# Moving the feature load and normalisation into the edge-list stage, and moving two runs of padding instructions

## The reference

```python
h = jnp.maximum(_layernorm(x, axis=-1), 0.0)
x = x + hypergraph_layer(h, edge_index, W1, b1, W2, b2)
h = jnp.maximum(_layernorm(x, axis=-1), 0.0)
x = x + edge_layer(h, src, dst, edge_weight1, eW1, eb1, ..., nW2, nb2)

# hypergraph_layer: twice, with a relu between
e = B_inv[:, None] * segment_sum((x @ W)[node_idx], edge_idx)
out = D_inv[:, None] * segment_sum(e[edge_idx], node_idx) + b

# edge_layer
e = silu(concat([h[row], h[col], dist]) @ eW1 + eb1)
e = silu(e @ eW2 + eb2)
agg = segment_sum(e, row)
out = silu(concat([h, agg]) @ nW1 + nb1) @ nW2 + nb2
```

## Time and profile before

| what | value |
|---|---|
| three runs | 9711.72, 9714.66, 9674.4 us (median 9711.72) |
| the profiled execution: time, span | 9704.83 us, 9703.1 us |
| PE busy, share of the span | 9097.1 us, 94% |
| DVE busy | 8012.9 us, 83% |
| ACT busy | 5832.8 us, 60% |
| POOL busy | 2410.2 us, 25% |
| granted TensorE clock, mean | 0.973 of full speed |

### The profile page before, as it was taken

How to read it: one execution, slowest core, us unless ns; L and a number is a source line. 1 busy time by engine, 2 the same in 40 slices (tenths; PEclk the granted TensorE clock), 3 DMA queues, 4 the chain that set the end, 5 groups by cost and what they waited for, 6 DMA issues and landing times. The chain is left out here.

```text
span 9703.1 us, 312435 instructions
## 1 busy us (share of the span) xinstructions
PE 9097.1 (94%) x105494; PEld 8224.5 (85%) x105494; DVE 8012.9 (83%) x25426; ACT 5832.8 (60%) x14221; POOL 2410.2 (25%) x3828
## 2 busy tenths in 40 slices
PE   1999999999999999999888899679999999999997
PEld 1888888888888887999888899669999999999995
DVE  6999999999999998577598888558888888888884
ACT  1888888888888887000177788335555555555553
POOL 2555545554555453000000000001111111111110
PEclk9999999999999999999799999769999999999998
DMA  2333333333333333766499999553333333333332
GB/s 58 91 90 91 93 93 91 90 93 92 92 89 93 92 92 105 196 190 190 119 224 223 215 247 248 109 146 95 92 91 92 95 93 94 89 94 95 91 93 72
DMA packets 849659, 1149.54 MB, mean 118 GB/s; under 512 B 204300, under 2 KB 585462, under 8 KB 848004
## 3 DMA queue, kind: packets, MB, share of 16 engines
q1 hardware_dynamic: 818806, 1112.73, 43.5%
q0 software_dynamic: 28224, 26.62, 1.1%
q10 hardware_dynamic: 1840, 0.53, 0.0%
HBM read 777.40 MB, written 361.77 MB: 117 GB/s over the span
## 5 line engine op out<-in xcount | busy, mean ns | idle before, releaser
L601 POOL TENSOR_SCALAR OH<-iot,kd 128x102 bf16<-128x102 bf16 x3440 | 1973.3, 592 | 1635.5 <-DVE ddc L912 1600.5
L855 ACT ACTIVATE RB<-PS 128x512 int16<-128x512 f32 x2401 | 1408.9, 592 | 534.6 <-PE PS L721 484.7
L2136 POOL DMA_INDIRECT Qx<-tab_q,tidx x294 | 423.3, 1440 | 5170.0 <-DVE skt L2170 2586.1
L1000 DVE TENSOR_SCALAR OU<-iot,SBk 128x256 bf16<-128x256 bf16 x4802 | 1379.5, 287 | 0.0
L1391 PE MATMUL wp<-AF,XS 128*128 128x256 f32 x9604 | 1213.9, 285 | 143.0 <-issue 110.7
L1391 PEld LDWEIGHTS wp<-AF,XS 128*128 128x128 f32 x9604 | 1167.5, 191 | 172.1 <-issue 171.0
L719 PE MATMUL PS<-OU 128*128 128x256 bf16 x4802 | 1188.0, 273 | 44.1 <-DVE OU L1000 30.3
L1417 ACT ACTIVATE AF<-RG 128x1536 fp32r<-128x1536 uint8 x686 | 1022.6, 1491 | 327.1 <-PE wp L1391 264.8
L737 PE MATMUL HP<-T3a,RB 128*128 128x193 bf16 x9604 | 1192.9, 247 | 1.6 <-ACT RB L855 1.6
L721 PE MATMUL PS<-OU 128*128 128x128 bf16 x9604 | 1190.9, 219 | 0.0
L2157 ACT ACTIVATE Z<-Zb 128x512 f32<-128x512 f32 x882 | 556.3, 631 | 1022.2 <-DVE Zb L2215 1022.2
(11 more groups left out here) (326 smaller groups left out, 17602.8 us busy)
## 6 DMA issues: line engine op xcount, KB each, us to landing
RG<-adjT SPq DMA_DIRECT2D x1372, 224.0 KB, 6.0
adj<-RB SPq DMA_DIRECT2D x343, 448.0 KB, 2.6
adjT<-RB SPq DMA_DIRECT2D x686, 224.0 KB, 3.3
RG<-adj SPq DMA_DIRECT2D x686, 224.0 KB, 4.5
sdb<-bk SPq DMA_DIRECT2D x196, 768.0 KB
sdb<-bk SPq DMA_DIRECT2D x98, 384.0 KB
sdb<-bk SPq DMA_DIRECT2D x98, 261.0 KB
WR<-wk SPq DMA_DIRECT2D x882, 9.0 KB
```

Of the source, the lines that this page charges most:

```text
L601: ins = e.tensor_scalar(OH[:, g * GT + k, :], iot1[:, 0:KEYS], kd[:, g * GT + k:g * GT + k + 1], None, ALU.is_equal)
L855: e.activation(RB[n % NSLOT][:, :, k, :].bitcast(i16), bank(u)[:, :].rearrange("p (a w) -> p a w", a=2), ACT.Copy, accum_out=gs[:, u:u + 1 ...
L1000: ins = e.tensor_scalar(o[:, x_, P:3 * P], iot1[:, :], SBk[:, KEYS + b:KEYS + b + 1], None, ALU.is_equal)
```

## The change

The feature block is gone. Its load, its normalisation and its split stand in the edge block now:

- SyncE issues the two feature loads first, as soon as VectorE has zeroed the tile's corner, and the edge lists behind them.
- VectorE normalises in place in `X0` (it wrote the top of `ACC` before), and then works out the keys.
- The split is no longer VectorE's: ScalarE casts the three parts into `T3a` (three `ACTIVATE` copies), GpSimd does the two subtractions, and semaphore `l_s` passes the work back and forth between them. The values are the same.
- `junkb` and `junka` now lie in `HI` and `tb_`, which are free by then.
- `spaced(e, SPACE1)` stands in the edge block, where TensorE has nothing else; `spaced(e, SPACE2)` in the residual block, ahead of TensorE's wait for `x_v`.

```diff
+        tz = ExitStack()
+        T3af = sbt(tz, "T3a", [P, BLK * W3], bf16)
...
+            X0 = sbt(st, "X0", [P, NB, F], fp32)
...
-            junkb = sbt(st, "junkb", [P, TI], bf16)
-            junka = sbt(st, "junka", [P, TI], bf16)
+            junkb = HI
+            junka = tb_[:, 0:TI // 2].bitcast(bf16)
...
                 @block.scalar
                 def _(e):
                     load_weights(e)
+                    norm.scalar(e)
+                    v = X0[:, 0:BLK, :]
+                    e.wait_ge(norm.steps, 8)
+                    e.activation(T3a[:, :, 0:F], v, ACT.Copy).then_inc(l_s, 1)
+                    e.wait_ge(l_s, 3)
+                    e.activation(T3a[:, :, F:2 * F], v, ACT.Copy).then_inc(l_s, 1)
+                    e.wait_ge(l_s, 5)
+                    e.activation(T3a[:, :, 2 * F:3 * F], v, ACT.Copy).then_inc(l_s, 1)
+
+                @block.tensor
+                def _(e):
+                    spaced(e, SPACE1)
 
                 @block.sync
                 def _(e):
+                    e.wait_ge(l_s, 1)
+                    load_x(e, X0, l_x)
                     e.wait_ge(s_c, 3)
                     load_edges(e, E["d"], dst, s_ld)
...
                 @block.vector
                 def _(e):
+                    e.memset(eps[:, :], 1e-5)
+                    e.memset(X0[:, 97:NB, :], 0.0).then_inc(l_s, 1)
                     e.memset(E["d"][:, :], PAD).then_inc(s_c, 1)
                     e.memset(E["s"][:, :], PAD).then_inc(s_c, 1)
                     e.memset(Wt[:, :], 0.0).then_inc(s_c, 1)
-                    e.memset(eps[:, :], 1e-5)
+                    e.memset(T3a[:, :, 3 * F:W3], 1.0)
+                    e.wait_ge(l_x, 32)
+                    norm.vector(e, X0, acc64, X0[:, :, :])
                     e.wait_ge(s_fill, 1)
...
                     e.tensor_copy(idb[:, :], idn[:, :])
+                    for n in range(2):
+                        v, a = X0[:, 0:BLK, :], n * F
+                        e.wait_ge(l_s, 2 * n + 2)
+                        e.tensor_tensor(v, v, T3a[:, :, a:a + F], ALU.subtract).then_inc(l_s, 1)
                     e.iota(pio[:, :], pattern=[[P, 2]], base=1, channel_multiplier=1, allow_small_or_imprecise_dtypes=True)
...
-        def split3(link, e, to, v, rest):
-
-            link(e.tensor_copy(to[:, :, 0:F], v))
-            link(e.tensor_tensor(rest, v, to[:, :, 0:F], ALU.subtract))
-            link(e.tensor_copy(to[:, :, F:2 * F], rest))
-            link(e.tensor_tensor(rest, rest, to[:, :, F:2 * F], ALU.subtract))
-            link(e.tensor_copy(to[:, :, 2 * F:3 * F], rest))
...
-                    def _(e):
-                        e.dma_start(X[:, 0:97, :], x[0:97 * P, :].rearrange("(b p) f -> p b f", p=P)).then_inc(l_x, 16)
-                        e.wait_ge(l_s, 1)
-                        e.dma_start(X[0:N_NODES - 97 * P, 97, :], x[97 * P:N_NODES, :]).then_inc(l_x, 16)
...
-                        norm.vector(e, X, acc64)
...
-                        split3(link, e, T3a, Hn[:, 0:BLK, :], X[:, 0:BLK, :])
...
-                        spaced(e, SPACE1)
                         e.wait_ge(c_init, 4)
                         ranks(0, 0)
...
                 @block.tensor
                 def _(e):
+                    spaced(e, SPACE2)
                     e.wait_ge(x_v, 14)
                     e.matmul(pov[:, 0:1], lhsT=onef[:, :], rhs=xov[:, 0:1], start=True, stop=True).then_inc(x_v, 1)
...
                     with e.If(fits(e)):
-                        spaced(e, SPACE2)
                         e.sem_inc(l_p, OFF)
```

More of the change, by code:

```diff
@@ L318, in gnn_kernel @@
         s_k, s_km = sem("s_k"), sem("s_km")
+        tz = ExitStack()
+        T3af = sbt(tz, "T3a", [P, BLK * W3], bf16)
+        T3a = T3af[:, :].rearrange("p (b f) -> p b f", f=W3)
+        l_x, l_s = sem("l_x"), sem("l_s")
+        norm = Norm("a")
         st = ExitStack()
         with st:
+            X0 = sbt(st, "X0", [P, NB, F], fp32)
             E = {"s": sbt(st, "E_s", [P, TI], i32), "d": sbt(st, "E_d", [P, TI + 1], i32)}
@@ L444, in _ @@
                         e.matmul(pk[:, 256:257], lhsT=onef[:, :], rhs=bad[:, :], start=True, stop=True).then_inc(s_km, 1)
-        def split3(link, e, to, v, rest):
-            link(e.tensor_copy(to[:, :, 0:F], v))
-            link(e.tensor_tensor(rest, v, to[:, :, 0:F], ALU.subtract))
-            link(e.tensor_copy(to[:, :, F:2 * F], rest))
-            link(e.tensor_tensor(rest, rest, to[:, :, F:2 * F], ALU.subtract))
-            link(e.tensor_copy(to[:, :, 2 * F:3 * F], rest))
-        tz = ExitStack()
-        with tz:
[L456 to L464, removed]
-                    def _(e):
-                        e.dma_start(X[:, 0:97, :], x[0:97 * P, :].rearrange("(b p) f -> p b f", p=P)).then_inc(l_x, 16)
-                        e.wait_ge(l_s, 1)
-                        e.dma_start(X[0:N_NODES - 97 * P, 97, :], x[97 * P:N_NODES, :]).then_inc(l_x, 16)
[L470 to L474, removed]
-                        norm.vector(e, X, acc64)
[L476 to L481, removed]
-                        split3(link, e, T3a, Hn[:, 0:BLK, :], X[:, 0:BLK, :])
-                    @block.scalar
-                    def _(e):
-                        norm.scalar(e)
+        with tz:
             p1 = ExitStack()
```

## The result

| | median of 20 runs | lowest to highest |
|---|---|---|
| before | 9712.49 us | 9674.3 to 9735.65 |
| after | 9672.49 us | 9639.84 to 9680.74 |

The ratio is 0.9957 with a 95% interval of 0.9948 to 0.9965: 0.43% faster, 40.0 us by the medians, and so within the 0.5% that I had called no change. The interval is 0.17% wide, so 20 runs of each kernel do tell a difference of 0.4% from none; that "about 0.5% is what a measurement can tell" was too cautious. The forecast was 9671, from 33.7 us.

A forecast was written before the change was run, and what follows sets the result against it. TensorE bounds the long stages (busy 9097.1 of 9703.1 us), VectorE alone the program's head. Front 57.0, less 26.8 waiting, plus 3.5 padding: 33.7 us off 9704.8 gives 9671, range 9637 to 9698.

The forecast's parts named there:

- Features land: Edge block's head: feature load issued at about 1.9, 17.4 us plus 1.3 for weights' loads, landing at 20.6 us.
- Normalisation: VectorE in the edge block, behind the feature load: the same eight instructions, 39.4 us, to 60.0.
- Edge lists: Lists' loads behind the features: SyncE reaches them at 16.7, they land at about 46, costing the path nothing.
- Keys and offsets: VectorE after normalisation: keys 48.8 us, offsets block with barrier 3.9, to 112.9; waiting for GpSimd's subtractions priced at 26.8.
- the two stream counts: GpSimd subtraction's length by streams passed in turn: 10.7 us for two, 16.0 for three; the middle, 13.4, taken.
- the two kinds: Keys' long VectorE instructions: two SBUF inputs or fast one-input, expected to wait for GpSimd; only the reduction at 73.99 is neither.
- The chunk block's start: VectorE's start of the chunk block, before at 169.94: near 140 with waiting, 113 without.
- SPACE1: 136 padding increments moved from chunk block to edge block: TensorE begins 13.3 us earlier, but the gain is 3.5 us.
- SPACE2: 52 padding increments, 8.0 us, moved out of the edge-layer block: gains nothing there and hides in the new place.
- no mutual waiting: Rival for VectorE beside GpSimd's subtractions: no or little waiting, 60.5 us off, 9644; chance 0.25.
- A slow subtraction: Rival for GpSimd's subtractions: at 5.2 ns an element VectorE is held 65 us, 9710, no change; chance 0.09.
- slower: Rival for GpSimd's subtractions: each over 54.5 us, two hold VectorE or the barrier 109 us, giving -48.5; chance 0.04.

The follow-up runs named there:

- The last experiment: Changed kernel with GpSimd's two subtractions moved to VectorE between the keys' instructions, and an early ScalarE square root to load its table; median 9659.65 us, ratio 0.9946.

## Why the prediction was right

Point by point, by its own steps.

1. *Features land:* 20.6 predicted, 21.34 measured. The load went out earlier than I had (1.24), and took 20.1 us instead of 18.7, 2.7 us more than the 17.4 of before. That is the size of the weights' whole share (2.6) and not of half, but no run separates the weights from the edge lists, which also stood behind the features, or from the scatter of the landing, 1.4 us over the traces.
2. *Normalisation:* 39.4 predicted; from 21.34 to 62.04 it is 40.7. The 1.3 us are ScalarE's table load. It used to run in the feature wait, where the window shows it as 1.24 us of ScalarE; in the changed kernel it runs only when the sum is ready, on the path. I had that row and didn't ask what its work was. The last experiment shows the term by removing it. The two rows of before, to be read against those at 49.06 and 50.84:

```profile
88.76 1.28 ACT L208 ACT_TABLE_LOAD   x1 [88.76 <-PEq L423]
134.37 0.78 DVE L202 RECIPROCAL ln_v<-ln_m 128x100 f32<-128x100 f32 x1 [0.52 <-ACT ln_m L208]
```

3. *Edge lists:* no wait behind the normalisation, as forecast. SyncE came to the lists at 18.17 (16.7 predicted), since the issue of the second feature load took 15.98 us instead of 13.89; its first store behind the lists goes out at 44.19 (they were to land at about 46).
4. *Keys and offsets:* from 62.19 to 133.75, 71.6 us, which is 48.8 and 22.8. The waiting was priced at 26.8. That each engine waits for the other's whole instruction was right, in both directions; the size was off by the length of a subtraction, 11.7 instead of 13.4 us (near the lower of the two stream counts, 10.7), and by the 0.3 us of each subtraction that VectorE did not wait (11.4 of 11.7). The prediction's "27.5 to 38 us won" for a subtraction of 16 to 10.7 us should have read 28.5 to 39.1 by its own terms (57.0 + 3.5 less twice the subtraction). It also called the reduction at 73.99 the only long instruction that is neither of the two kinds; L393 at 79.41 (3.51 us, one input) is another. Nothing hung on that, as the subtractions got in at once. The offsets block with its barrier took 4.5 instead of 3.9 us.
5. *The chunk block's start* follows as 112.9 + 26.8 = 139.7 by the prediction and was 138.25.
6. *SPACE1:* 3.5 predicted, 2.6 at chunk 1's one-hots and about 2 at its first count. That GpSimd's one-hots, and not TensorE, pace chunk 0 was right.
7. *SPACE2:* nothing predicted, 4.5 us measured from the transpose, 4.9 from the block's start. This step failed: "In its old place it ended at 6468.0 and TensorE then waited for a DMA until 6476.2, so removing it gains nothing". That row says what TensorE waited for, not what the DMA had waited for. Behind the padding stood `sem_inc(l_p, OFF)`, and SyncE's first load of the block waits for `l_p`; the padding was a link of the chain that ended in the very wait I took for its cover. Before, that load went out at 6468.08, right behind the padding's end, 8.0 us into the block; in the changed kernel it goes out 3.7 us into it. The two kernels with the padding on either side of the increments show it. In the new place it hides, as forecast: TensorE waited 37.9 us for `xov`.

The sum: 31.7 of front instead of 30.2, about 2.6 for SPACE1 instead of 3.5, 4.5 for SPACE2 instead of 0, and 0.6 between the block's start and the first one-hot make 39.4, and the medians differ by 40.0. So 33.7 was low by 6 us. The landmarks account for them, with the caution that the medians' difference has an interval of its own (34 to 51 us by the ratio) and the landmarks come from one execution of each. That the median then came within 2 us of 9671 owes something to my having taken the sum from an execution 8 us below the median of before.

Of the rivals, *no mutual waiting* is refuted by the stretched instructions and by the kernel without subtractions, which has that rival's front: 115.62, where steps 1, 2 and 4 without waiting and with what they measured give 115.5. *A slow subtraction* and *slower* fall with its 11.7 us. The chunk loop kept its period: from chunk 1's to chunk 48's first count it is 3506.5 us before and 3503.1 after, 0.07 us a turn.

The rule of the Trainium skill ("SBUF — State Buffer", who interferes with whom) holds here in the half that no row of before could show: VectorE is the one who waits, 13.22 us instead of 1.84 in its fast kind and 14.89 instead of 3.52 with two inputs. The fast kind waits for a fill too: 6.92 us instead of 1.84 beside a fill of 5.42.

## What to carry to other kernels

Work handed from VectorE to GpSimd isn't hidden beside VectorE instructions with two SBUF inputs or of the fast one-input kind: here 23.8 us of split were taken off VectorE and 22.8 us of waiting put on it, and the profile calls that waiting busy time, so look for instructions that are longer than their kind. ScalarE did take work over for nothing: beside its casts VectorE's instructions kept their length. Before an instruction run is priced at nothing because its engine waits afterwards, ask who waits for what stands behind it in its list: a semaphore increment behind padding can hold the very DMA that the engine waits for in the end.

## What the hardware showed that was not expected

- The waiting between VectorE and GpSimd was expected for the subtractions. What was not: it is there for GpSimd instructions that read nothing, 5.1 us of a 5.4 us fill, and a 0.13 us `iota` becomes 1.79 us behind VectorE's fast kind.
- The diff works in the first 200 us and at the head of the edge-layer block; the scatter comes from elsewhere. The block of one small linear layer that stands ahead of the residual block takes 75 to 77 us at a mean clock of 0.51 to 0.54 in ten of the twelve profiled executions, 44 or 45 us at 0.98 or 0.99 in two (with the split on VectorE, and with the table early). The block in the changed kernel, and in the one with the split on VectorE:

```profile
6127.00:6203.00 76.00, 71.77 (x304) 57.91 (x304) 11.39 (x29) 14.93 (x26) 0.00 (x0) 0.52 0.00 1
```

```profile
6134.00:6179.00 45.00, 40.82 (x309) 34.01 (x308) 11.30 (x28) 15.02 (x26) 0.00 (x0) 0.98 0.01 1
```

  The same matmuls (some records are missing from either trace) run near one or the other of the two levels, 1.2 and 2.4 GHz, 31 us apart, though no edit touches that block; in the wide hops right ahead of it the clock was 0.99 either way. The wide hops, whose DMA engines are 99% busy or more, took between 1356 and 1385 us in the four traces in which they were read. Each of these two spreads is about three quarters of the whole change. What puts TensorE's clock on the one or the other level in that block stays open; it was not tried.
